# Attention probabilities turned in 32 by 32 blocks on VectorE, sigma_k spread by ScalarE

## What is computed

```python
def step(carry, seg):
    mem, z = carry
    qq, kk, vv = seg
    sigma_q = elu(qq) + 1.0
    scores = where(causal_mask, einsum('bhsk,bhtk->bhst', qq, kk) / scale, -inf)
    att_dot = softmax(scores) @ vv
    att_mem = sigma_q @ mem / (sigma_q @ z)
    sigma_k = elu(kk) + 1.0
    delta = vv - sigma_k @ mem / (sigma_k @ z)
    mem_new = mem + einsum('bhsk,bhsv->bhkv', sigma_k, delta)
    z_new = z + sigma_k.sum(over the tokens)
    att = beta * att_mem + (1.0 - beta) * att_dot
    return (mem_new, z_new), att @ Wo
```

## Time and profile before

| | |
|---|---|
| median of 3 runs | 691.12 us |
| lowest, highest | 688.59, 693.03 us |
| the profiled execution | 688.85 us |
| its span | 687.1 us |
| TensorE busy | 630.4 us, 92% |
| VectorE busy | 409.9 us, 60% |
| ScalarE busy | 332.6 us, 48% |
| GpSimd busy | 248.2 us, 36% |

### The profile page before, as it was taken

How to read it: one execution, slowest core, us unless ns; L and a number is a source line. 1 busy time by engine, 2 the same in 40 slices (tenths; PEclk the granted TensorE clock), 3 DMA queues, 4 the chain that set the end, 5 groups by cost and what they waited for, 6 DMA issues and landing times. The chain is left out here.

```text
span 687.1 us, 12129 instructions
## 1 busy us (share of the span) xinstructions
PE 630.4 (92%) x4182; PEld 551.5 (80%) x4182; DVE 409.9 (60%) x1047; ACT 332.6 (48%) x812; POOL 248.2 (36%) x283
## 2 busy tenths in 40 slices
PE   3999999999999999999999897688999958996997
PEld 2789889988989979989989796576777756985775
DVE  6849687388386388485484735694223279545444
ACT  2658677467577467576476551322444311201221
POOL 3718420156120167120120211606777505200474
PEclk9999999999999999999999999899999979996899
DMA  8101200001100000000000402794334270009541
GB/s 266 57 2 32 62 1 1 9 11 53 39 1 2 8 31 31 8 0 0 9 1 1 109 1 70 277 412 120 104 105 101 77 262 34 0 1 349 188 129 41
DMA packets 26513, 51.59 MB, mean 75 GB/s; under 512 B 4478, under 2 KB 15712, under 8 KB 26464
## 3 DMA queue, kind: packets, MB, share of 16 engines
q1 hardware_dynamic: 19456, 35.74, 15.1%
q0 software_dynamic: 4896, 13.12, 6.8%
q10 hardware_dynamic: 2112, 2.10, 0.9%
HBM read 41.76 MB, written 10.09 MB: 75 GB/s over the span
## 5 line engine op out<-in xcount | busy, mean ns | idle before, releaser
L907 DVE RECIPROCAL denominators<-readings 128x2 f32<-128x2 f32 x120 | 20.1, 167 | 113.4 <-PE readings L581 112.9
L786 ACT ACTIVATE memory_reading<-readings,denominators 64x128 f32<-64x128 f32 x240 | 73.8, 356 | 26.1 <-DVE denominators L907 24.6
L581 PEld LDWEIGHTS readings<-memory_copy,sigma 128*128 128x128 f32 x480 | 70.6, 191 | 9.5 <-ACT memory_copy L777 1.7
L591 PE MATMUL memory<-minus_delta,sigma_k_tokens 128*128 128x129 f32 x480 | 75.0, 278 | 3.5 <-DVE minus_delta L913 3.4
L468 POOL TENSOR_TENSOR scores<-scores,score_max 128x512 f32<-128x512 f32 x16 | 16.7, 1045 | 168.2 <-DVE score_max L928 168.2
L581 PE MATMUL readings<-memory_copy,sigma 128*128 128x129 f32 x480 | 73.7, 275 | 1.6 <-ACT memory_copy L777 1.6
L913 DVE SCALAR_TENSOR_TENSOR minus_delta<-readings,denominators,v 64x128 f32<-64x128 f32 x224 | 69.0, 348 | 4.0
L591 PEld LDWEIGHTS memory<-minus_delta,sigma_k_tokens 128*128 128x128 f32 x480 | 63.2, 191 | 6.3 <-DVE minus_delta L913 5.0
L777 ACT ACTIVATE memory_copy<-memory 128x258 f32<-128x258 f32 x120 | 46.9, 391 | 42.5 <-PE memory L591 42.3
L630 PE MATMUL ahead<-wo,attT 128*128 128x256 f32 x256 | 64.9, 398 | 1.2 <-DVE attT L942 1.2
L1217 POOL DMA_INDIRECT xs_e<-rows_e,gather_at_e x46 | 44.6, 970 | 52.1 <-DVE gather_at_e L1631 18.2
(11 more groups left out here) (288 smaller groups left out, 1466.2 us busy)
## 6 DMA issues: line engine op xcount, KB each, us to landing
weights_e<-experts SPq DMA_DIRECT2D x24, 608.0 KB, 12.0
xn<-L_attn_Wq SPq DMA_DIRECT2D x4, 512.0 KB, 3.9
wo<-L_attn_Wo SPq DMA_DIRECT2D x1, 2048.0 KB, 13.2
rows_e<-xn ACTq DMA_DIRECT2D x4, 512.0 KB, 9.4
xn<-L_attn_Wv SPq DMA_DIRECT2D x3, 512.0 KB, 3.9
xn<-L_attn_Wk SPq DMA_DIRECT2D x3, 512.0 KB, 3.8
x<-L_attn_x SPq DMA_DIRECT2D x4, 256.0 KB, 4.0
x<-L_attn_x SPq DMA_DIRECT2D x2, 512.0 KB, 3.7
```

What stands on the lines that cost most here:

```text
L581: last = pe.matmul(KQ[g][:, hh * MC:(hh + 1) * MC], sqk[:, GROUP * g + hh, pair, 2 * par:2 * par + 2, :], mz[g][:, hh, :], start=True, sto ...
L591: last = pe.matmul(MM[g][:, hh * MC:(hh + 1) * MC], skt[:, GROUP * g + hh, pair, :], dl[g][par][:, hh, :], start=False, stop=True, skip_gr ...
L786: last = act.activation(read[rows, half, GROUP * g + hh, pair, :], KQ[g][rows, hh * MC:hh * MC + DK], ACT.Copy, scale=nr[g][rows, hh:hh + 1])
```

## The change

GpSimd now multiplies all 128 partitions of a pair's exponentials in place, one multiplication instead of two. VectorE transposes them, in 32x32 blocks, straight into the operand of the local product, `pT`, whose other blocks are set to zero once. One instruction takes one 32x32 block of each of the eight 64x64 matrices in a row of tiles: 32 partitions by 8 by 32 elements, eight instructions a pair. TensorE's transposes and ScalarE's copies of them go. The local products stand at m = 11 and 14 instead of 10 and 14, their scaling at m = 12 and 15. The copy of sigma_k into the operand of the readings (L892) goes from VectorE to ScalarE, at m = 11 to 14, and TensorE also waits for it at the start of a stage; a key's sigma now waits for the spread of the key two before it, whose buffer it takes.

```diff
-        probs = norm.xn[1][:, TPH:NT, :].rearrange("p t d -> p (t d)").rearrange("p (t c) -> p t c", c=P)
...
-        pTs = [x_space[:, (2 + i) * HALF:(3 + i) * HALF] for i in range(2)]
+        pT = [space.rearrange("p (i c) -> p i c", c=P)
+              for space in (x_space[:, 2 * HALF:4 * HALF], norm.xn[1][:, TPH:NT, :].rearrange("p t d -> p (t d)"))]
...
+        LOCAL_AT = (11, 14)
+        TURN_PROBS_AT = {8: ((0, range(0, 3)),), 9: ((0, range(3, 6)),), 10: ((0, range(6, 8)), (1, range(0, 1))),
+                         11: ((1, range(1, 3)),), 12: ((1, range(3, 5)),), 13: ((1, range(5, 8)),)}
...
-                    pool.memset(probs[:, :, :], 0.0).then_inc(consts_set, 1)
+                    pool.wait_ge(norm.xn_done, NT)
+                    for pp in range(2):
+                        pool.wait_ge(consts_set, 13 + pp)
+                        pool.memset(pT[pp][:, :, :], 0.0).then_inc(consts_set, 1)
...
-                    for par in range(2):
-                        rows = slice(par * SEG, (par + 1) * SEG)
-                        pool.tensor_tensor(probs[rows, :, par * SEG:(par + 1) * SEG], sm[pp][rows, :, :],
-                                           rs[pp][rows, :].unsqueeze(2).to_broadcast([SEG, NT, SEG]), ALU.mult)\
-                            .then_inc(p_ready, 1)
+                    pool.tensor_tensor(sm[pp][:, :, :], sm[pp][:, :, :],
+                                       rs[pp][:, :].unsqueeze(2).to_broadcast([P, NT, SEG]), ALU.mult)\
+                        .then_inc(p_ready, 1)
...
-                def turn_probs(n, pp, hh):
-                    for t in range(TPH):
-                        last = pe.transpose(L[hh][:, t * P:(t + 1) * P], probs[:, hh * TPH + t, :], ident[:, :])
-                    last.then_inc(pT_ready, 1)
...
                     for t in range(TPH):
                         last = pe.matmul(L[hh][:, t * P:(t + 1) * P], v[:, half * TPH + t, h * DK:(h + 1) * DK],
-                                         pTs[hh][:, t * P:(t + 1) * P], start=True, stop=True)
+                                         pT[pp][:, hh * TPH + t, :], start=True, stop=True)
...
-                    if m == 8:
-                        pe.wait_ge(p_ready, 4 * n + 2)
...
-                        turn_probs(n, 0, 0)
-                        turn_probs(n, 0, 1)
-                    if m == 12:
-                        pe.wait_ge(p_ready, 4 * n + 4)
                         for hh in range(2):
-                            pe.wait_ge(bt_copied, 4 * n + hh + 1)
-                            turn_probs(n, 1, hh)
-                    if m in (10, 14):
-                        for hh in range(2):
-                            local(n, half, (m - 10) // 4, hh)
+                    if m in LOCAL_AT:
+                        pp = LOCAL_AT.index(m)
+                        pe.wait_ge(pT_ready, 2 * n + pp + 1)
+                        if pp:
+                            pe.wait_ge(bt_copied, 4 * n + 2)
...
+                            local(n, half, pp, hh)
...
+                        pe.wait_ge(sk_spread, 4 * n + 4)
...
-                def copy_probs(n, pp):
-                    for hh in range(2):
-                        act.wait_ge(pT_ready, 4 * n + 2 * pp + hh + 1)
-                        act.activation(pTs[hh][:, :], L[hh][:, :], ACT.Copy).then_inc(pTs_ready, 1)
+                def spread_sigma_k(n, half, h):
+
+                    act.wait_ge(sigma_ready, 8 * n + h + 5)
+                    tiles = slice(half * TPH, (half + 1) * TPH)
+                    act.activation(sqk[:, h, tiles, 0:4:3, :],
+                                   sk[h % 2][:, :].rearrange("p (t a c) -> p t a c", a=2, c=SEG), ACT.Copy)\
+                       .then_inc(sk_spread, 1)
...
-                    if m in (9, 13):
-                        copy_probs(n, (m - 9) // 4)
-                    if m in (11, 15):
-                        if m == 11 and not half:
+                    if 11 <= m < 11 + HQ and not (last and half):
+                        spread_sigma_k(n + 1, 1 - half, m - 11)
+                    if m - 1 in LOCAL_AT:
+                        pp = LOCAL_AT.index(m - 1)
+                        if not (pp or half):
...
-                                                 op0=ALU.max, op1=ALU.add).then_inc(sk_ready, 1)
-                        dve.wait_ge(sk_ready, 4 * n + h + 1)
...
-                        last = dve.tensor_copy(sqk[:, h, tiles, 0:4:3, :], by_segment(sk[h % 2][:, :]))
+                            dve.wait_ge(sk_spread, 4 * n + u - 5)
...
+                def turn_probs(n, pp, part, before):
+                    if part[0] == 0:
+                        dve.wait_ge(p_ready, 2 * n + pp + 1)
+                        if before:
+                            dve.wait_ge(bt_ready, 4 * n - 2 + 2 * pp)
+                    for block in part:
+                        par, q, k = block // 4, block // 2 % 2, block % 2
+                        of, to = par * SEG + q * SEG // 2, par * SEG + k * SEG // 2
+                        last = dve.transpose(pT[pp][to:to + SEG // 2, :, of:of + SEG // 2],
+                                             sm[pp][of:of + SEG // 2, :, k * SEG // 2:(k + 1) * SEG // 2])
+                    if part[-1] == 7:
+                        last.then_inc(pT_ready, 1)
...
+                    for pp, part in TURN_PROBS_AT.get(m, ()):
+                        turn_probs(n, pp, part, behind)
```

More of the change, by code:

```diff
@@ L489, in turn @@
                     for half in range(2):
-                        n, before = 2 * it + half, not (first and not half)
-                        if before:
-                            pool.wait_ge(p_ready, 4 * n)
+                        n = 2 * it + half
                         for pp in range(2):
                             shift_scores(n, pp)
-                        pool.wait_ge(shifted, 2 * n + 2)
-                        probabilities(n, 0, before)
+                        probabilities(n, 0)
                         if not (half or last):
-                            pool.wait_ge(p_ready, 4 * n + 2)
                             split_next(it, 0)
@@ L652, in slot @@
                         turn_reading(1 - half, h)
-                    if m == 8:
-                        pe.wait_ge(p_ready, 4 * n + 2)
-                        if behind:
+                    if m in LOCAL_AT:
[3 more added lines that the diff above has]
+                            pe.wait_ge(bt_copied, 4 * n + 2)
+                        elif behind:
                             pe.wait_ge(att_ready, 4 * n)
@@ L722, in _ @@
                 wait_copied("project", QUERY - 1)
-                pe.wait_ge(consts_set, 14)
+                pe.wait_ge(consts_set, 15)
                 seed(0)
@@ L825, in slot @@
                         exp_scores(n, m // 5)
-                    if m in (9, 13):
-                        copy_probs(n, (m - 9) // 4)
-                    if m in (11, 15):
-                        if m == 11 and not half:
+                    if 11 <= m < 11 + HQ and not (last and half):
[3 more added lines that the diff above has]
+                        if not (pp or half):
                             act.wait_ge(beta_q_set, it + 1)
-                        scale_local(n, half, (m - 11) // 4)
+                        scale_local(n, half, pp)
                 def turn(it, first, last):
@@ L849, in _ @@
                 for i, (what, u) in enumerate(AT_START):
+                    if what == "turn":
+                        spread_sigma_k(0, 0, u)
                     (copy_sigma_k if what == "turn" else copy_projection)(0, 0, u, norm_banks[i % 4])
@@ L886, in sigma @@
                             dve.wait_ge(skt_ready, 4 * n + u - 5)
-                        dve.scalar_tensor_tensor(out=sk[h % 2][:, :], in0=natural, scalar=0.0, in1=e[u % 3],
-                                                 op0=ALU.max, op1=ALU.add).then_inc(sk_ready, 1)
-                        dve.wait_ge(sk_ready, 4 * n + h + 1)
-                    tiles = slice(half * TPH, (half + 1) * TPH)
-                    if i:
-                        last = dve.tensor_copy(sqk[:, h, tiles, 0:4:3, :], by_segment(sk[h % 2][:, :]))
+                            dve.wait_ge(sk_spread, 4 * n + u - 5)
+                        last = dve.scalar_tensor_tensor(out=sk[h % 2][:, :], in0=natural, scalar=0.0, in1=e[u % 3],
+                                                 op0=ALU.max, op1=ALU.add)
                     else:
+                        tiles = slice(half * TPH, (half + 1) * TPH)
                         last = dve.scalar_tensor_tensor(out=sqk[:, h, tiles, 1:3, :], in0=by_segment(natural), scalar=0.0,
@@ L917, in step, with mask_scores @@
                     last.then_inc(dl_ready[g], 1)
-                def mask_scores(n, pp, before):
-                    if before:
-                        dve.wait_ge(p_ready, 4 * n - 2 + 2 * pp)
+                def turn_probs(n, pp, part, before):
[10 more added lines that the diff above has]
```

(8 more changed lines are left out.)

12 lines of the change are left out of this document (3 added, 9 removed).

## The result

The changed kernel takes 719.62 us (median of 4 runs, 716.37 to 721.06) against 689.86 us for the kernel before in the same comparison: a ratio of 1.0423 with an interval of 1.0392 to 1.0453, so 4.2% slower. The forecast was 706, the range 693 to 719. The direction is right; the loss is 30 us where 16 were worked out. The profiled execution took 719.8 us (span 718.0).

The account below looks back on a forecast made before the run. It took TensorE and VectorE to be in balance, VectorE without slack in slots 7 to 9. Stage losses 4.0 + 5.6 + 6.5 = 16.1 us on 688.85 or 691.12 gave 705.0 or 707.2, forecast 706; range 698 to 714, wider 693 to 719.

Parts of the forecast that it names:

- The four rules: Attention slots: reciprocal at least 0.65 us after reading, update 0.85 after reciprocal, next reading 1.83 after update; VectorE's slot sums its work.
- the price of 0.45: VectorE's block transposes in slots 8 to 13: 0.45 us each, bounded by 0.29 and 0.70.
- the three kinds of stage: Stages 1, 3, 5, 6: 1.0 us longer each; 2 and 4, with POOL splitting weights: 2.8 each; stage 0: 6.5.
- the wait of 0.75 for the second local product: Stages 2 and 4: TensorE's second local product waits 0.75 us, a term of the 2.8 forecast for each.
- rival B's second half: POOL's weight splitting stretches ten transposes of three stages by 0.4 us: 12 us more, 718; chance of the whole rival 0.15.
- its first half: Each VectorE transpose costs 0.70 us: 17.5 us more, 723; chance of the whole rival 0.15.
- rivals A and C: A: transposes fill VectorE's idle time, 678 us, chance 0.08. C: transposes run at COPY's rate, 0.29 us, 695 us, chance 0.14.
- Nothing later waits: Stage 3 behind slot 12: the reading of slot 13 comes 1.0 us later than before, and no further wait follows.
- a wash: ScalarE loses four copies of 128x512 and gains four spreads of the same size, with no net cost.
- with the wait that they bring: TensorE's eight transposes in slot 12 take 1.15 us including their wait; counted within the 1.9 us saved a stage.
- The range: Own range 698 to 714 us; 693 to 719 takes in the forecast, rival C and the near edge of rival B.

Follow-up runs that it names:

- the one with the filler: The changed kernel plus 13 useless transposes of the identity on TensorE before its wait for the first pair's turned probabilities in slot 11: 712.07 us, ratio 1.0315.
- the local products moved: The changed kernel with the local products put behind the slot's projection and turn of sigma_k in slots 11 and 14: 698.14 us, ratio 1.0121.
- both moves: The changed kernel with local products at the end of slots 11 and 14, and output projection ahead of the turn in slots 12 and 13: 691.89 us, 1.006.

## Why the prediction was right in its direction and short in size

The measured change of each stage (from the windows) splits by three pairs of kernels: the clock's part is the changed kernel less the one with the filler; the turn's part is the local products moved less both moves, at a clock of 1.00 in both; the rest is what the forecast worked out. Stage 0 has no output projection to put ahead, so its turn's part is read from its slot 13 instead, which grew from 2.60 to 3.36. The turn there waited for VectorE before the change (first row), and waits for ScalarE now (second row); it waits the same 1.80 in the kernel without most of the transposes:

```profile
71.87 0.63 PE L568 MATMUL ahead<-ident,sigma_k 128*128 128x128 f32 x4 [1.08 <-DVE sigma L892]
```

```profile
77.66 0.66 PE L565 MATMUL ahead<-ident,sigma_k 128*128 128x128 f32 x4 [1.80 <-ACT sigma_k_tokens L758]
```

| stage | forecast | measured | clock | turn of sigma_k | rest |
|---|---|---|---|---|---|
| 0 | 6.5 | 8.25 | 1.07 | 0.76 | 6.4 |
| 1 | 1.0 | 3.87 | 1.63 | 1.03 | 1.2 |
| 2 | 2.8 | 5.91 | 2.90 | 1.09 | 1.9 |
| 3 | 1.0 | 2.08 | 0.00 | 1.03 | 1.05 |
| 4 | 2.8 | 4.01 | 1.08 | 1.09 | 1.8 |
| 5 | 1.0 | 3.71 | 1.62 | 1.03 | 1.1 |
| 6 | 1.0 | 2.25 | -0.02 | 1.04 | 1.2 |
| sum | 16.1 | 30.1 | 8.3 | 7.1 | 14.7 |

**The four rules, the price of 0.45, the three kinds of stage.** Right: 14.7 us against 16.1, and stage 0 lengthened most. Stage 7 and what follows it took 308.5 us against 307.3 before, the start 0.4 less: no more than executions differ there, so nothing speaks against the 0 that was forecast. In stages 2 and 4 the forecast was 0.9 to 1.0 us too much each; the wait of 0.75 for the second local product, which it had put there, did not come (that product waits once in all, 1.8 in stage 0). The transposes themselves were not stretched, 423 to 443 ns beside whatever GpSimd does, so rival B's second half falls, and its first half with rivals A and C by the price.

The Trainium skill ("Vector Engine (DVE) Microarchitecture Reference", 3.8 The reshape front-end and per-opcode configuration) has the 32x32 transpose at one element per cycle per lane. The trace does not contradict it: 435 ns for 256 elements a lane stands beside 409 ns for the 256 that BN_STATS reads and 426 ns for COPY's 512; a rate by the cycle no run here shows.

**"Nothing later waits", and ScalarE "a wash".** Wrong, 7.1 us, and the first step that failed. The forecast booked the eight transposes of slot 12 as 1.15 us saved, "with the wait that they bring", and did not ask what that wait was for: ScalarE's copy, which the turn behind them needs and still waits for when they are gone. It also counted ScalarE's copies by their number and not by their slots: the four copies that went stood in slots 9 and 13, the spreads that came stand in 11 to 14, and the scaling moved from slot 11 to 12, in front of the copy that the next turn waits for (236.16 and 237.31, above).

**The clock.** Missing, 8.3 us: the second step that failed. The forecast priced each wait by its length. Of the seven stages with waits of up to 1.4 us for minus_delta and 1.4 to 1.9 for the local product in slots 10 and 11, five lost another 1.1 to 2.9 us each to a lower granted clock, two lost none. Why stages 3 and 6 kept it is not settled: stage 3 has the waits of stage 1 to 0.1 us, and in the kernel with only the output projection moved it is stages 1 and 3 that kept it, while stage 6 lost it (0.97).

**The range.** It was made from the price of a transpose and from the rivals. The two causes outside the sum had no place in it: 719.6 less 8.3 and 7.1 is 704.2, close to the 706 that was forecast. That the direction came out right is the mechanism's doing; that the time is only 0.6 beyond the range is luck, since half of the loss comes from steps that the forecast did not have.

## What to carry to other kernels

An engine with a 40% idle share has room only where it idles: find the slots, and move the chain that feeds the work so that it may stand there, before moving the work. Before an instruction is taken off the bounding engine, see what it covers: the next wait behind it is due as soon as it is gone, and a second engine that gets its place in the same slots makes it longer. A wait on TensorE should be covered by any useful work that can go ahead of it; here that gave 21 us for waits of 13, since the clock's 8 went with them.

## What the runs showed of the hardware that I had not expected

In stage 1 of the changed kernel TensorE waits 1.40 us, 2 us after a wait of 0.73. Right behind that the granted clock fell from 1.00 to 0.50 (from 2.4 to 1.2 GHz); the windows of 2 us show 0.70, 0.50 and 0.95. With 13 small useless matmuls in the place of the second wait it stayed at 1.00 in every stage. With the same waits, to 0.1 us, it fell in some stages and not in others.
